# Two transposes of a routed-FFN stage moved from TensorE to VectorE by way of DRAM

## The reference, cut to what matters

```
y   = (shared_ffn(x) + gate1 * expert_a(x) + gate2 * expert_b(x)) / 3     # top 2 of 8, per token
sel = argmax(softmax(gelu(y[:, -1] @ Wp1 + bp1) @ Wp2 + bp2))             # one big expert per batch
z   = gelu(y @ W1[sel] + b1[sel]) @ W2[sel] + b2[sel]
x1  = x + y + 0.3 * (z @ Wo + bo)
dx  = shift(x1) - x1                                                      # the row before; row 0: cond
xr  = x1 + dx * maa_r ;  r = xr @ w_recept.T                              # sigmoid later
xk  = x1 + dx * maa_k ;  hashed experts: relu(xk @ w_key)**2 @ w_value    # 16 experts, 256 rows each
out = x1 + a recurrence over the 32 batches on sigmoid(r) * hashed(xk)
```

## Time and profile before

| | us |
|---|---|
| median of 3 runs (2495.56 to 2496.51) | 2496.48 |
| the profiled execution, its own time | 2494.64 |
| its span in the profile | 2492.9 |
| TensorE busy, share of the span | 97% |
| mean granted TensorE clock, of full speed | 0.993 |

### The profile page before, as it was taken

One profiled execution on the slowest core, in us unless ns is written; L12 is line 12 of the kernel. 1 busy time (PEld: TensorE's weight loads), 2 busy tenths in 40 slices (PEclk: granted clock), 3 DMA queues, 4 the chain that ended last, 5 costly groups with the idle time before them and its releaser, 6 DMA issues.

```text
span 2492.9 us, 40630 instructions
## 1 busy us (share of the span) xinstructions
PE 2429.3 (97%) x12307; PEld 2021.7 (81%) x12309; DVE 1195.2 (48%) x1833; ACT 901.0 (36%) x1459; POOL 548.4 (22%) x498
## 2 busy tenths in 40 slices
PE   8999999999999899999999989999999999999999
PEld 4778888888899688888888868888888888888877
DVE  5555455325343243443444357777753333333356
ACT  3233333216555322222222236666652222222234
POOL 1100000002222266666666610000001111111100
PEclk9999999999999899999999999999999999999999
DMA  8698888407466533364345256666642111111135
GB/s 287 203 336 301 304 320 312 164 18 275 164 214 248 178 114 115 109 254 120 106 126 178 93 197 223 235 242 225 233 171 77 51 44 45 51 46 46 42 101 185
DMA packets 165172, 420.68 MB, mean 169 GB/s; under 512 B 31379, under 2 KB 67699, under 8 KB 148578
## 3 DMA queue, kind: packets, MB, share of 16 engines
q1 hardware_dynamic: 137810, 322.08, 37.2%
q0 software_dynamic: 19072, 61.66, 8.1%
q10 hardware_dynamic: 8208, 35.88, 3.8%
HBM read 558.71 MB, written 144.80 MB: 282 GB/s over the span
## 4 chain that ended last, share of the span: by engine, by line
PE 68%; DMA 2%; DVE 2%; issue 2%; ACT 1%; SPq 0%; POOL 0%; another core or an unknown queue 0%; DVEq 0%; POOLq 0%; ACTq 0%
PE s_g L99 8%; PE s_g L101 8%; PE s_g L100 8%; PE s_h_ps L99 5%; PE s_h_ps L101 5%; PE s_h_ps L100 5%; PE s_z_ps L99 2%; PE s_z_ps L101 2%; PE s_z_ps L100 2%; PE s_o_ps L99 2%; PE s_o_ps L100 2%; PE s_o_ps L101 1%; PE s_h L99 1%; PE s_h L100 1%; PE s_h L101 1%
## 5 line engine op out<-in xcount | busy, mean ns | idle before, releaser
L99 PE MATMUL s_g<-wx_hi,s_x_hi 128*128 128x512 f32 x512 | 203.3, 397 | 2.3 <-DVE s_x_lo L2339 1.6
L101 PE MATMUL s_g<-wx_hi,s_x_lo 128*128 128x512 f32 x512 | 199.8, 390 | 0.0
L100 PE MATMUL s_g<-wx_lo,s_x_hi 128*128 128x512 f32 x512 | 199.4, 390 | 0.0
L2234 POOL DMA_INDIRECT s_y<-mid_hash_out,first_rec x32 | 31.5, 985 | 736.0 <-DMA mid_hash_out<-s_o 392.7
L2045 DVE TENSOR_TENSOR s_w_lo<-s_w_raw,s_w_hi 128x1024 fp32r<-128x1024 f32 x124 | 146.4, 1221 | 46.6 <-ACT s_w_hi L1974 45.4
L99 PE MATMUL s_h_ps<-s_x_hi,s_w_hi 128*128 128x256 f32 x512 | 145.7, 285 | 7.1 <-DVE s_x_lo L2077 7.1
L99 PE MATMUL s_g<-s_u,s_c_hi 128*128 128x512 f32 x384 | 150.2, 391 | 1.6 <-PEq L1858 1.6
L101 PE MATMUL s_g<-s_u,s_c_lo 128*128 128x512 f32 x384 | 149.9, 390 | 0.0
L100 PE MATMUL s_g<-s_u,s_c_hi 128*128 128x512 f32 x384 | 149.4, 389 | 0.0
L101 PE MATMUL s_h_ps<-s_x_hi,s_w_lo 128*128 128x256 f32 x512 | 145.5, 284 | 0.0
L100 PE MATMUL s_h_ps<-s_x_lo,s_w_hi 128*128 128x256 f32 x512 | 145.5, 284 | 0.0
(11 more groups left out here) (411 smaller groups left out, 6747.3 us busy)
## 6 DMA issues: line engine op xcount, KB each, us to landing
s_half<-mid_w ACTq DMA_DIRECT2D x124, 2048.0 KB
s_w_raw<-in_w SPq DMA_DIRECT2D x64, 512.0 KB, 6.1
mid_w<-s_x_grp SPq DMA_DIRECT2D x32, 1024.0 KB, 5.8
mid_w<-s_pool_b SPq DMA_DIRECT2D x32, 1024.0 KB, 4.9
s_half<-mid_w SPq DMA_DIRECT2D x32, 1024.0 KB
s_w_raw<-in_w2h SPq DMA_DIRECT2D x16, 2048.0 KB, 9.1
s_w_raw<-in_w1h SPq DMA_DIRECT2D x15, 2048.0 KB, 7.5
mid_routed<-s_o_sb SPq DMA_DIRECT2D x72, 256.0 KB
```

The source lines that it names most:

```text
L99: pe.matmul(out, a_hi, w_hi, start=first, stop=False, skip_group_check=True)
L100: pe.matmul(out, a_hi, w_lo, start=False, stop=False, skip_group_check=True)
L101: return pe.matmul(out, a_lo, w_hi, start=False, stop=last, skip_group_check=True)
L2234: pool.indirect_dma_start(y[:], None, d["hash_out"], bass.IndirectOffsetOnAxis(rec[:, SLOTH:SLOTH + 1].bitcast(U32), 0)).then_inc(S["y_in" ...
```

## The change

In the FFN stage y (batches 1 to 31) and xr (batches 0 to 29) are no longer turned by PE. They are written by quarter, stored to DRAM by SP, loaded back by quarters and turned by VectorE. y comes back into the buffer of z and is turned into `ty_ps`; xr comes back into its own buffer and is turned into a new SBUF tile `xrt`. `combine` writes y in four pieces. All steps of the stage but `gather`, `combine`, `load_rec`, `load_shared` and `load_x` get one more lag, so that y is combined two batches ahead of its `up`. `add_base` is cut in two, x + y and + bo. The transfers wait: `store_y` on y, `load_y` on the turn of the z before and on the store, `store_xr` on xr, `load_xr` on its store, all through SP's one list. `z_add` waits until y is out of z.

`turn_quarters` now writes runs of 32 neighbouring columns in place of every fourth column. What makes up for it are rows "dealt" on their way to DRAM: store position 4t+s takes row 32s+t. The indirect store of xk stays as it was, and the hashed stage's result rows are dealt back when they are stored. The recurrent stage keeps the old form under the name `turn_dealt_quarters`.

```diff
+def dealt(rows):
+
+    return rows.rearrange("(t s) c -> s t c", s=4)
...
+def turn_dealt_quarters(dve, dst, src):
+
+    return dve.transpose(dst.rearrange("p k (t s) -> p k s t", s=4), src.rearrange("p (s k a) -> p k s a", s=4, a=32))
...
 def turn_quarters(dve, dst, src):
 
-    return dve.transpose(dst.rearrange("p k (t s) -> p k s t", s=4), src.rearrange("p (s k a) -> p k s a", s=4, a=32))
+    return dve.transpose(dst.rearrange("p k (s t) -> p k s t", t=32), src.rearrange("p (s k a) -> p k s a", s=4, a=32))
...
+            def store_y(i, n, turn):
+                if isinstance(i, int) and i == 0:
+                    return
+                wait_apart(sp, S["y"], i + 1)
+                sp.dma_start(dealt(y_rows[n]), y[:]).then_inc(S["y_sent"], 16)
+
+            def load_y(i, n, turn):
+                if isinstance(i, int) and i == 0:
+                    return
+                wait_apart(sp, S["tz"], i - 1)
+                wait_apart(sp, S["y_sent"], i * 16)
+                load_by_quarters(sp, z[:], y_rows[n], S["y_quarters"])
+
+            def store_xr(i, n, turn):
+                if isinstance(i, int) and i >= NB - 2:
+                    return
+                wait_apart(sp, S["xr"], i + 1)
+                sp.dma_start(dealt(xr_rows[n]), xr[:]).then_inc(S["xr_sent"], 16)
+
+            def load_xr(i, n, turn):
+                if isinstance(i, int) and i >= NB - 2:
+                    return
+                wait_apart(sp, S["xr_sent"], i * 16 + 16)
+                load_by_quarters(sp, xr[:], xr_rows[n], S["xr_quarters"])
...
-            software_pipeline(sp, NB, [(0, load_rec), (2, load_b2), (1, load_b1), (3, store_x1),
-                                       (0, load_shared), (0, load_x), (5, store_r)], 2)
+            software_pipeline(sp, NB, [(0, load_rec), (5, store_xr), (3, load_b2), (5, load_xr), (2, load_y), (2, load_b1), (1, store_y),
+                                       (4, store_x1), (0, load_shared), (0, load_x), (6, store_r)], 2)
...
+            def add_y(i, n, turn):
                 pool.wait_ge(S["x_in"], i * 16 + 16)
                 pool.wait_ge(S["y"], i + 1)
                 wait_for(pool, S["base"], i)
-                pool.tensor_tensor(base_part[:], x[:], y[:], ALU.add).then_inc(S["x_plus_y"], 1)
+                if isinstance(i, int) and i == 0:
+                    pool.tensor_tensor(base_part[:], x[:], y[:], ALU.add).then_inc(S["x_plus_y"], 1)
+                else:
+                    pool.tensor_tensor(in_order(base_part[:]), in_order(x[:]), by_quarter(y[:]), ALU.add).then_inc(S["x_plus_y"], 1)
+
+            def add_base(i, n, turn):
                 pool.wait_ge(S["x_plus_y"], i + 1)
                 wait_for(pool, S["x1"], i - 1)
                 pool.tensor_tensor(base[:, n], base_part[:], bo[:], ALU.add).then_inc(S["base"], 1)
...
-                    wait_for(pool, S["txr"], i)
-                    pool.tensor_tensor(xr[:], k_part[:], x1[:], ALU.add).then_inc(S["xr"], 1)
+                    wait_for(pool, S["xrt"], i)
+                    if is_next_to_last(i):
+                        pool.tensor_tensor(xr[:], k_part[:], x1[:], ALU.add).then_inc(S["xr"], 1)
+                    else:
+                        pool.tensor_tensor(by_quarter(xr[:]), in_order(k_part[:]), in_order(x1[:]), ALU.add).then_inc(S["xr"], 1)
...
-            software_pipeline(pool, NB, [(0, gather), (1, add_base), (3, mix)], 2)
+            software_pipeline(pool, NB, [(0, gather), (2, add_base), (1, add_y), (4, mix)], 2)
...
             software_pipeline(act, NB, [
-                (2, load_hashed), (2, part_hi(z_hi, tz_ps, "tz", "mmo", 1, "z_hi")), (1, gelu(0)), (0, load_w1), (1, h_hi(0)), (1, gelu(1)),
-                (0, load_w2), (1, h_hi(1)), (3, hashed_hi(0, 2)), (4, copy_r), (3, xr_hi_),
-                (3, hashed_hi(2, DC)), (0, y_hi_), (0, load_second)], 2)
+                (0, first_weights), (3, load_hashed), (3, part_hi(z_hi, tz_ps, "tz", "mmo", 1, "z_hi")), (2, gelu(0)), (1, load_w1), (2, h_hi(0)), (2, gelu(1)),
+                (1, load_w2), (2, h_hi(1)), (4, hashed_hi(0, 2)), (5, copy_r), (4, late(xr_hi_, True)),
+                (4, hashed_hi(2, DC)), (0, first_y_hi), (1, y_hi_), (1, load_second), (4, late(xr_hi_, False))], 2)
...
+                wait_for(dve, S["ty"], min(i + 2, NB) if isinstance(i, int) else i + 2)
...
-                wait_for(dve, S["ty"], i)
+                if isinstance(i, int) and i < 2:
+                    wait_for(dve, S["ty"], i)
+                else:
+                    dve.wait_ge(S["y_sent"], i * 16 - 16)
...
-                dve.scalar_tensor_tensor(y[:], routed[1][:], rec_f[:, n, GATE2:GATE2 + 1], y_part[:],
-                                         ALU.mult, ALU.add).then_inc(S["y"], 1)
...
+                for k in range(DC):
+                    last_part = dve.scalar_tensor_tensor(
+                        by_quarter(y[:])[:, k], in_order(routed[1][:])[:, k], rec_f[:, n, GATE2:GATE2 + 1],
+                        in_order(y_part[:])[:, k], ALU.mult, ALU.add)
+                last_part.then_inc(S["y"], 1)
+
+            def turn_y(i, n, turn):
+                if isinstance(i, int) and i == 0:
+                    return
+                dve.wait_ge(S["y_quarters"], i * 16)
+                dve.wait_ge(S["y_lo"], i)
+                turn_quarters(dve, ty_ps[:], z[:]).then_inc(S["ty"], 1)
...
+            def turn_xr(i, n, turn):
+                if isinstance(i, int) and i >= NB - 2:
+                    return
+                dve.wait_ge(S["xr_quarters"], i * 16 + 16)
+                wait_for(dve, S["xr_lo"], i)
+                turn_quarters(dve, xrt[:], xr[:]).then_inc(S["xrt"], 1)
...
+                src = tz_ps if is_next_to_last(i) or is_last(i) else xrt
...
             software_pipeline(dve, NB, [
-                (2, z_add), (1, h_add(0)), (2, part_lo(z_lo, tz_ps, z_hi, "z_hi", "z_lo")), (0, combine), (1, h_add(1)),
-                (1, h_lo(0)), (2, x1_), (1, h_lo(1)), (3, hashed_lo(0, 2)),
-                (3, xr_lo_), (2, last_mix), (3, hashed_lo(2, DC)), (0, make_shift),
-                (0, y_lo_)], 2)
+                (3, z_add), (2, h_add(0)), (3, part_lo(z_lo, tz_ps, z_hi, "z_hi", "z_lo")), (0, combine), (2, h_add(1)),
+                (2, h_lo(0)), (3, x1_), (2, h_lo(1)), (4, hashed_lo(0, 2)),
+                (4, late(xr_lo_, True)), (3, last_mix), (4, hashed_lo(2, DC)), (0, make_shift),
+                (0, first_y_lo), (1, turn_y), (1, y_lo_), (4, turn_xr), (4, late(xr_lo_, False))], 2)
...
             software_pipeline(pe, NB, [
-                (1, find_weights), (1, up(0)), (2, turn(z, "z_add", tz_ps, "xr_lo", 1, "tz")), (1, up(1)), (1, turn_h(0)),
-                (4, receptance_at(True)), (2, times_wo), (1, turn_h(1)), (3, turn_xr(True)), (2, shift_last),
-                (4, receptance_at(False)),
-                (3, turn_xr(False)), (0, turn_y), (1, down)], 2)
+                (2, find_weights), (2, up(0)), (3, turn_z), (2, up(1)), (2, turn_h(0)),
+                (5, receptance_at(True)), (3, times_wo), (2, turn_h(1)), (4, turn_xr(NB - 2)), (3, shift_last),
+                (5, receptance_at(False)),
+                (4, turn_xr(NB - 1)), (0, turn_y), (2, down)], 2)
...
-                    sp.dma_start(d["hash_out"][bass.ds(e * CAP + m * P, P)], o_sb[m][:]).then_inc(S[f"o_out{m}"], 16)
+                    sp.dma_start(dealt(d["hash_out"][bass.ds(e * CAP + m * P, P)]), o_sb[m][:]).then_inc(S[f"o_out{m}"], 16)
```

More of the change, by code:

```diff
@@ L1331, in stage_ffn @@
                  "w1_in0 w1_in1 w2_in00 w2_in01 w2_in10 w2_in11 "
-                 "part_y y base x_plus_y ty y_hi y_lo half_y half_ty half_y_hi half_y_lo h_ps h_add gelu th h_hi "
-                 "h_lo mm2 z_add tz z_hi z_lo mmo x1 x1_out prev_in dx k_part xk r_part xr ~xk_sent txr xr_hi "
+                 "part_y y y_sent y_quarters base x_plus_y ty y_hi y_lo half_y half_ty half_y_hi half_y_lo h_ps h_add gelu th h_hi "
+                 "h_lo mm2 z_add tz z_hi z_lo mmo x1 x1_out prev_in dx k_part xk r_part xr xr_sent xr_quarters xrt ~xk_sent txr xr_hi "
                  "xr_lo mmr r_ready ~r_out hashed_in hashed_hi shift shifted ~first_hash0 ~first_hash1")
@@ L1487, in gather @@
                                             ).then_inc(S[f"routed{k + 1}_in"], 16)
-            def add_base(i, n, turn):
+            def add_y(i, n, turn):
                 pool.wait_ge(S["x_in"], i * 16 + 16)
@@ L1533, in load_w1 @@
                                           cond=unused).then_inc(S[name], 16)
-                    return
-                if isinstance(i, int) and i == 1:
+            def load_w1(i, n, turn):
+                if isinstance(i, int) and i < 2:
                     return
@@ L1581, in part_hi, with first_y_hi @@
                 return stage
-            def y_hi_(i, n, turn):
+            def first_y_hi(i, n, turn):
                 if isinstance(i, int) and i == 0:
@@ L1588, in y_hi_ @@
```

(28 more changed lines are left out.)

40 lines of the change are left out of this document (31 added, 9 removed).

## The result

The changed kernel takes 2714.88 us (median, 2711.33 to 2716.84) against 2496.48: a ratio of 1.0874 [1.0855, 1.0893]. That is 218 us slower where 8 us faster was forecast, and far outside the range.

A forecast was written before the change was run, and what follows sets the result against it. TensorE (PE), busy for 97% of the span, was taken as the bound. The terms -26.5 - 9 + 15.5 + 9.5 + 2 = -8.5 us gave 2486.1 us profiled, 2488 for the median (chance 0.43), range 2474 to 2504.

The forecast's parts named there:

- Turns off PE: FFN stage: 31 turns of y and 30 of xr leave PE, 0.435 us each, -26.5 us.
- The way through DRAM in a common round: FFN rounds: y and xr pass through SP's gaps, y ready at 14 to 16 us; cost 0, slack only 2 us.
- Rival C: FFN rounds: turn_y waits for a quarter load landing later than 16 us into the round; 2518 us, chance 0.13.
- Combine: FFN stage: y written in four pieces takes 1.4 us, h_add(1) comes 0.6 later under 1.5 of cover; cost 0.
- The hashed stage: Contiguous turn_quarters near 0.72 us closes most of PE's wait for h_lo; -9 us (bounds 0 and -10).
- B: Rival: contiguous turns are no faster in SBUF, so the 9 us go; 2497 us, no change, chance 0.15.
- The start: FFN stage's start: b1 of batch 0 and combine(2) come later, first down at 876.4 not 863.37; +15.5 us (12 to 18).
- The expert changes: While new weights load, xr's store and load, then y's load, delay up(14): +9.5 us (0 to 13); second change +2.
- theory F: From the experiments, not the prediction: transfers with outermost dimension 4 are served by 4 of the 16 DMA engines.
- Rival D: Expert changes cost double, each of a quarter load's pieces may wait its turn: +11.5 to 14, 2501 us, chance 0.11.

The follow-up runs named there:

- run 4: The changed kernel with plain stores of y, xr and the hashed result, and each quarter load cut into four of 32 partitions that deal the rows; 2506.27 us.
- run 13: run 9 with the combination of every batch but the first moved to the very end of VectorE's round; 2650.47 us.
- run 6: run 4 with the combination moved in VectorE's list from ahead of h_add(1) to behind h_lo(1); 2516.52 us.
- run 1: The kernel before with only the change's part in the hashed stage (contiguous turn, dealt stores); 2511.82 us, ratio 1.0063.
- run 2: The kernel before with the hashed stage's contiguous turn, plain stores, and each quarter load cut into four of 32 partitions dealing the rows; 2480.99 us, ratio 0.9934.
- run 9: run 4 with y and xr regrouped in DRAM: one store of 512-byte pieces, one plain load, the strided turn; 2488.88 us, ratio 0.9968.
- run 15: run 2 with xr alone sent through DRAM, regrouped, and y still turned by TensorE; 2477.51 us, ratio 0.9923, and again 2475.98, 0.9916.
- run 7: run 6 with the load of b1 moved ahead of the loads of xr and y in SP's list; 2540.55 us.
- run 16: run 15 with xr's load moved behind b1 and the store of x1 in SP's list; 2496.88 us, ratio 1.0000.
- run 5: The changed kernel with xr's load moved behind the store of y in SP's list; 2693.22 us.

## Why the prediction was wrong

**Turns off PE, right.** -0.87 a round was forecast; with the transfers on all engines the rounds are 17.88 (18.78 - 17.88 = 0.90), and 18.27 with one of the two turns gone.

**The way through DRAM in a common round, the step that failed.** "SP is free between b2 and the b1 of the next batch" and "`load_y` ... is issued at 4 to 6" took the gaps of SP's old list as room. It came at 12.7. I priced the load rightly (8, measured 8.75) from the one row of its form. But I gave the store no price, though the load of xr has to follow its landing (6.03 us from issue to issue), and a dealt store has the same outermost dimension of 4. Nor did I ask what slow transfers do to their neighbours: prev and x1 of the same queue run behind them. What was put at "slack only 2 us" and a cost of 0 was a loop of 24 us: a common round came out at 23.9 and not 17.9, about 171 us over 29 rounds. Rival C had the place, the wait of `turn_y`, and its sign; its condition ("once the load lands later than 16 us into the round") is what happened, with 21.5 us. At 0.13 and 2518 us it was far too small in both, and it put the lateness down to two loads sharing a queue; the two loads do follow each other, but on four engines. I took the 8 us as a price, did not ask why 256 KB need it, and left the contradiction with the rule of 512 bytes (the Trainium skill, "DMA: Bandwidth & Descriptors", section "Specifications") without a cause. The trace of before had it; this window, not read then, lies in the quarter load of the earlier trace rows and shows the same share and rate:

```profile
1468.00:1470.00 2.00, 0.98 (x3) 0.26 (x1) 0.00 (x0) 0.60 (x1) 0.00 (x0) 0.65 0.29 87
```

Run 4 moved the same bytes in 5.4 us.

**Combine, right** in its cost of 0 for common rounds (its four pieces took 1.17 us in run 13, 1.4 was said), and misplaced as a risk: not its own length matters but what it waits for (runs 4, 6, 13).

**The hashed stage, wrong by its store.** The turn fell to 0.70 as forecast (B is refuted), but -9 became +16 (run 1), because the change deals the rows in a store on 4 engines and this delays the quarter loads behind it. With plain stores and four-way loads the median falls by 14.9 (run 2), more than the -10 I had set as the bound; in the profiled executions it is 13.1, of which 10.9 lie behind round 31. As run 2 changed the loads too, it doesn't confirm the 9 for the turn.

**The start, right in place, and in size with full engines only.** There rounds 0 and 1 cost +15.2 (run 4: 47.35 against 32.18) where +15.5 stood, and `down` starts at 877.67 where 876.4 was said. In the changed kernel it is +21.5, beyond the bound of 18, since y of batch 1 also came late (load issued 878.57, turned 887.88):

```profile
870.49 0.69 DVE L1692 TENSOR_TENSOR s_h_pre<-s_h_ps,s_b 128x512 f32<-128x512 f32 x1 [13.60 <-DMA s_b<-in_b]
...
878.57 0.63 SPq L106 DMA_DIRECT2D s_z<-mid_y_rows  x1
...
887.88 0.73 DVE L136 STREAM_TRANSPOSE s_ty_ps<-s_z 128x512 f32<-128x512 f32 x1 [6.22 <-DMA s_z<-mid_y_rows]
```

b1 came at 870.49; 868.5 to 869.5 was said.

**The expert changes, mis-sized even without theory F.** +9.5 and +2 were forecast. In run 4 rounds 13, 14 and 25 have 32.1 us over a common round where the kernel before has 3.2, so +29; in run 9 +18, in run 15 +8 (+11 in the second profile). The forecast followed one chain, xr's store to y's load, and in run 4 TensorE's longest waits there, 2.40 and 6.15 us, are for gelu: b1, moved behind the loads and so behind the new weights, and the combination that waits for shared rows. Rival D doubled the sum to 23 and came nearer, but by luck: no run tested its mechanism, pieces that wait their turn.

That the rest at the changes is the weights' traffic meeting transfers that the order of one queue places badly is what runs 6, 7 and 16 suggest; none of them removed it, and weights spread over more rounds were not tried.

## What to carry to other kernels

Before a transfer is priced, look at the outermost dimension of both its sides, and read the DMA share while it runs alone: here 0.25 to 0.29 at 86 to 90 GB/s said that four engines did the work of sixteen. Regroup the rows so that both sides begin with 128. A step that is moved onto a queue with waits in it must be followed once round the whole loop (prev, xr, its store, its load, y, prev): here rounds of 23 to 24 us were such loops, and taking a wait out of an in-order list handed it to what stood behind it in runs 5, 6, 13 and 16. Of two similar halves of a change one can pay and the other not: xr through DRAM takes 0.5 us off each common round and gains some 4 us at best, y, which needs a batch more of lead, loses 11 to 13 (2488.9 of run 9 against 2477.5 and 2476.0 of run 15). Whether it is y's lead or its two transfers that costs this was not separated.

## What the runs showed that was not expected

A dealt store and a quarter load still in flight slowed plain transfers of the same queue: SP needed 6.15 us to hand over the two copies into prev in run 5, 1.6 in the changed kernel's round, where the quarter loads had nearly ended, and 1.54 before. VectorE's turn in SBUF depends on the stride of its writes (0.70 against 1.09 us for 128x512), while into PSUM both forms take 0.72. After the stop of 4.20 us before 1382.30 the granted clock read 0.50 in the windows from 1382 to 1388, where matmuls took 0.79 instead of 0.39; so a stop costs more than its length. The common stops from round 4 on are 3.9 us in the mean and those rounds some 5.9 us longer than 17.9, which leaves about 2 us a round for the clock, an estimate.
